# A mixture-of-experts block on one core: y's permit ahead of the gathers, and a weight load that waits for a gather

## The chip, the core and the metric

The kernel runs on one core of a Trainium2 chip. The metric is the device time of one launch in microseconds; runs of the kernel before gave 407.37, 409.26 and 410.68, so the median is 409.26.

## What is computed

The reference is a convolutional attention block over two images of 256 channels and 1024 positions, followed by a dense-looking feed-forward layer with 8 experts in which each of the 2048 tokens has a score for its two best experts and zero for the rest. Only the second part is touched by the change:

```
gate = softmax(xt @ Wg);  topv, topi = top_k(gate, 2);  topv = topv / (sum(topv) + 1e-06)
scores = zeros((T, E)).at[arange(T)[:, None], topi].set(topv)
for e in range(E):
    h = gelu(xt @ W1[e] + b1[e], approximate=False)
    out = out + (h @ W2[e] + b2[e]) * scores[:, e:e + 1]
```

with T = 2048 tokens of 256 values, E = 8, W1 256x1024 and W2 1024x256 for each expert, all in float32. The result is t + out, where t holds the tokens and xt is their layer norm.

## The kernel before

After the attention part (until about 150 us) the kernel sorts the (token, expert) pairs by expert into blocks of 128 rows. A tile is two blocks of one expert; an expert with an odd number of blocks begins with one tile of three. The number of tiles is only known at run time: VectorE writes first tile, end tile and flags of each expert into `bounds`, and each engine reads them into registers (`expert_bounds`, L339). In this run there are 17 tiles, numbered 0 to 16: tiles 0 to 2 are expert 0, 3 to 5 expert 1, 6 expert 2, 7 to 9 expert 3, 10 expert 4, 11 and 12 expert 5, 13 expert 6, 14 to 16 expert 7. Tiles 0 and 11 have three blocks.

Every float32 operand is split into a high and a low part, and each product is three matmuls (hi x hi, lo x hi, hi x lo).

One tile t, engine by engine:

- TensorE (`tile`, L1621): four of the eight first-layer column groups, then second and first layer in turns, then `turn_x(t + 1)` (L1575, transposes at L1572), which waits for `x_gathered` of tile t+1 and transposes the gathered rows `xg` into PSUM; then the last four groups of the second layer. In what follows "the turn in tile t" is this one.
- ScalarE (L813): gelu of each group twice, to h_raw (L820) and h_hi (L823). In the first tile of expert e it also copies the high part of the weights of expert e+1 out of `w_raw` (L833).
- VectorE (L1215): h_lo (L1221) of each group; after the first group of tile t it scales the y of tile t-1 by the scores (`y_scaled`, L1206, y_out at L1212), for which it waits on `y_free`; in an expert's first tile it makes w_lo (L1230); then x_lo (L1203) and y_sum (L1239).
- POOL, that is GpSimd (`tile`, L554): it keeps the scores of tile t+1 (L532, after that gather has landed), waits for the turn in tile t (`xg_turned`), and gathers the rows of tile t+2 into `xg` with three indirect DMAs (`gather`, L515, idx_in at L517, DMAs at L523). Then it waits until every earlier add has landed (`y_added`), copies the destinations into idx_out (L565) and gives `y_free`. When y_out is there (`y_weighted`) it issues two or three indirect DMAs that add y_out to the output rows (L573), and moves the scores on (L537).
- SyncE (L397 to L404): the weights of each expert, two DMAs of 1 MB (`load_expert`, L347), into `w_raw[e % 2]`. The load of expert e waits for `w_split`, that is for the low parts of expert e-2, which VectorE finishes at the end of the first tile of expert e-3; the load of expert 2 waits for the first gather too.

The semaphore of a DMA counts when the transfer has landed, not when it was issued.

Of the kernel before, what the change touches and what calls it, by code (L numbers as in the profile page):

```python
# [34 lines left out]
HJ = H // P  # L35
# [4 lines left out]
WIDE = 3  # L40
# [12 lines left out]
def metaformer_kernel(nc, x_tok_d, q1_d, q2_d, k1_d, k2_d, v_d, o_d, aff_d, og_d, ob_d,  # L53
                      wg_d, w1_d, b1_d, w2_d, b2_d, out_d):
    ctx = ExitStack()
    with ctx:
# [3 lines left out]
        def sem(name):  # L60
            return ctx.enter_context(nc.semaphore(name))
# [223 lines left out]
        bounds_ready = sem("bounds_ready")  # L285
# [7 lines left out]
        x_gathered = sem("x_gathered")  # L293
        idx_in_set = sem("idx_in_set")
        idx_out_set = sem("idx_out_set")
        xg_turned = sem("xg_turned")
# [9 lines left out]
        scores_kept = sem("scores_kept")  # L306
# [6 lines left out]
        w_split = sem("w_split")  # L313
# [25 lines left out]
        def expert_bounds(eng, e):  # L339

            word = eng.value_load(bounds[0:1, 0, bass.ds(e, 1)], min_val=8, max_val=264 * TMAX + 7)
            why = "VectorE counts at most TMAX tiles"
            first = nc.s_assert_within(word // 256, 0, TMAX - 1, skip_runtime_bounds_check_because=why)
            after = nc.s_assert_within(word % 256 // 8, 1, TMAX, skip_runtime_bounds_check_because=why)
            return first, after, word % 8 // 4, word % 2, word % 4 // 2

        def load_expert(sp, e):  # L347
            raw = w_raw[e % 2]
            sp.dma_start(raw[:, 0:KC * H].rearrange("p (k h) -> p k h", k=KC),
                         w1_d[e].rearrange("(k p) h -> p k h", p=P)).then_inc(w_loaded[e % 2], 16)  # L350
            sp.dma_start(raw[:, KC * H:].rearrange("p (j d) -> p j d", j=HJ),
                         w2_d[e].rearrange("(j p) d -> p j d", p=P)).then_inc(w_loaded[e % 2], 16)


        @block.sync
        def _(sp):
            def load_rows(u):
                sp.dma_start(x1[:, u * BLKU:(u + 1) * BLKU, :],
                             x_tok_d[u * UNIT:(u + 1) * UNIT, :].rearrange("(p j) c -> p j c", j=BLKU)
                             ).then_inc(x_loaded[u], 16)  # L360

            load_rows(0)
            load_rows(1)
            sp.dma_start(w_q1[:, :, :], q1_d.rearrange("(k p) o -> p k o", p=P)).then_inc(wq_loaded, 16)
            load_rows(2)
            load_rows(3)
            sp.dma_start(w_q2[:, :], q2_d).then_inc(wq_loaded, 16)
            sp.dma_start(aff[:, :], aff_d).then_inc(wq_loaded, 16)
            for dst, src in ((w_k1, k1_d), (w_v, v_d), (w_g, wg_d)):
                sp.dma_start(dst[:, :, :], src.rearrange("(k p) o -> p k o", p=P)).then_inc(conv_loaded, 16)  # L370
            for dst, src in ((w_k2, k2_d), (w_o, o_d),
                             (og, og_d.partition_broadcast(P)), (ob, ob_d.partition_broadcast(P))):
                sp.dma_start(dst[:, :], src).then_inc(conv_loaded, 16)
            sp.dma_start(b1t[:, :], b1_d).then_inc(bias_loaded, 16)
            load_expert(sp, 0)

            sp.wait_ge(pv_ready, GROUPS)
            sp.dma_start(b2b[:, :], b2_d.partition_broadcast(P)).then_inc(bias_loaded, 16)

            def store_rows(half):  # L380
                sp.wait_ge(xn2_ready, (4, 8)[half])
                sp.wait_ge(xn2_more, (4, 8)[half])
                sp.wait_ge(scores_ready, half + 1)
                sp.dma_start(xs_d[half * HALF * P:(half + 1) * HALF * P, :]
                             .rearrange("(u p j) c -> p u (j c)", p=P, j=BLKU),
                             xn2[:, half * HALF:(half + 1) * HALF, :].rearrange("p (u j) c -> p u (j c)", j=BLKU)
                             ).then_inc(xs_stored, 16)

            store_rows(0)

            sp.wait_ge(x1_ready, NBLK)
            sp.dma_start(out_d[0:TOK, :].rearrange("(u p j) c -> p u (j c)", p=P, j=BLKU),
                         x1[:, :, :].rearrange("p (u j) c -> p u (j c)", j=BLKU)).then_inc(x1_stored, 16)
            store_rows(1)

            sp.wait_ge(lg_ready, NBLK // 2)
            load_expert(sp, 1)  # L397
            for e in range(2, E):

                sp.wait_ge(w_split, HJ * (e - 1))  # L400
                if e == 2:
                    for i in range(WIDE):
                        sp.wait_ge(first_gathered[i], 16)
                load_expert(sp, e)  # L404


        @block.gpsimd
        def _(pool):
# [106 lines left out]
            def gather(n):  # L515

                pool.tensor_copy(idx_in[:, :], row_in[:, bass.ds(n, 1), :].rearrange("p a w -> p (a w)")  # L517
                                 ).then_inc(idx_in_set, 1)
                pool.wait_ge(idx_in_set, n + 1)
                pool.sem_inc(gathers_begun, 1)  # L520
                for i in range(WIDE):
                    done = first_gathered[i] if isinstance(n, int) and n == 0 else x_gathered
                    pool.indirect_dma_start(xg[:, i, :], None, xs_d,  # L523
                                            bass.IndirectOffsetOnAxis(ap=idx_in[:, i:i + 1], axis=0)
                                            ).then_inc(done, 16)

            def keep_scores(n):

                if not (isinstance(n, int) and n == 0):
                    pool.wait_ge(x_gathered, n * (16 * WIDE))  # L530
                pool.sem_inc(scores_begun, 1)
                pool.tensor_copy(score_next[:, :, :], xg[:, :, C:]).then_inc(scores_kept, 1)  # L532

            def move_scores(n):
                pool.wait_ge(scores_kept, n + 1)
                pool.sem_inc(scores_begun, 1)
                pool.tensor_copy(score[:, :, :], score_next[:, :, :]).then_inc(scores_moved, 1)  # L537
# [16 lines left out]
            def tile(t, e, block, width):  # L554


                pool.wait_ge(scores_moved, t + 1)
                keep_scores(t + 1)
                pool.wait_ge(scores_kept, t + 2)
                pool.wait_ge(xg_turned, t + 2)  # L560
                gather(t + 2)


                pool.wait_ge(y_added, block * 16 + 16)
                pool.tensor_copy(idx_out[:, :], row_out[:, bass.ds(t, 1), :].rearrange("p a w -> p (a w)")  # L565
                                 ).then_inc(idx_out_set, 1)
                pool.wait_ge(idx_out_set, t + 1)
                pool.sem_inc(y_free, 1)

                pool.wait_ge(y_weighted, t + 2)  # L570
                pool.sem_inc(adds_begun, 1)
                for i in range(width):
                    pool.indirect_dma_start(out_d, bass.IndirectOffsetOnAxis(ap=idx_out[:, i:i + 1], axis=0),  # L573
                                            y_out[:, i, :], None, compute_op=ALU.add).then_inc(y_added, 16)
                move_scores(t + 1)

            for e in range(E):
                _, t1, odd, more, _ = expert_bounds(pool, e)

                odd1 = pool.value_load(bounds[0:1, 1, e:e + 1], min_val=0, max_val=E)  # L580
                with pool.If(odd):
                    tile(t0, e, t0 * 2 + odd0, WIDE)
                with pool.Else():
                    tile(t0, e, t0 * 2 + odd0, 2)
                with pool.If(more):
                    with pool.Fori(t0 + 1, t1) as t:
                        tile(t, e, t * 2 + odd1, 2)
                t0 = t1
                odd0 = odd1
# [6 lines left out]
        def _(act):  # L596
# [255 lines left out]
            for e in range(E):  # L852
                _, t1, odd, more, _ = experts[e]
                with act.If(odd):
                    tile(t0, e, WIDE, True)
                with act.Else():
                    tile(t0, e, 2, True)
                with act.If(more):
                    with act.Fori(t0 + 1, t1) as t:
                        tile(t, e, 2, False)  # L860
                t0 = t1
# [821 lines left out]
```

## Time and profile before

| | us |
|---|---|
| median of 3 runs (lowest, highest) | 409.26 (407.37, 410.68) |
| the profiled execution | 408.46 |
| its span | 406.7 |
| TensorE busy | 362.1 (89%) |
| VectorE busy | 257.4 (63%) |
| ScalarE busy | 254.4 (63%) |
| GpSimd (POOL) busy | 188.2 (46%) |

Times in the trace are us from the start of the span. The span is what the profiled execution shows of the program; its device time is 1.8 us longer. A row of a timeline gives start, length, engine, line and instruction, and in brackets how long the engine stood idle before it and what ended that. TensorE's clock was granted at full speed throughout the expert part. The DMA issues on SyncE's queue are marked SPq.

### The profile page before, as it was taken

Reading aid. Unit: us, or ns where it says so; the run is one execution under the profiler, and the core shown is the slowest. Engines: PE = TensorE matmul, PEld = TensorE weight load, DVE = VectorE, ACT = ScalarE, POOL = GpSimd, SP = SyncE. Lnnn points to the kernel's source line nnn. Section 1 sums busy time; section 2 is a strip of 40 time slices with the busy share of each in tenths; the row PEclk is TensorE's granted clock in tenths of the full one; section 3 lists DMA queues with packets and bytes.
Section 4 is the critical chain, followed back from the end, with each engine's and each line's share of the span. In section 5 each row is a group of like instructions: output and inputs, shape, how many; then the busy total and the mean of one; then the engine's idle time right before and its main releaser. Section 6 shows DMA issues by size and latency. Waiting matters only on the chain.

```text
span 406.7 us, 8244 instructions
## 1 busy us (share of the span) xinstructions
PE 362.1 (89%) x2500; PEld 324.9 (80%) x2501; DVE 257.4 (63%) x650; ACT 254.4 (63%) x555; POOL 188.2 (46%) x232
## 2 busy tenths in 40 slices
PE   5989978999999796999999899898999999899950
PEld 4435456887879686899999798898989999899950
DVE  5858388788767996554467347784457854935530
ACT  2496657669557764756667466786567855865520
POOL 5800000002025655435666556685657556766553
PEclk9999999999999878999999999999999999999995
DMA  7810000000002773718325631658224714232342
GB/s 272 262 39 2 0 1 2 0 2 0 1 16 92 309 267 95 245 58 229 61 49 133 169 63 42 161 146 266 54 52 90 210 42 71 36 66 55 54 65 27
DMA packets 22965, 38.62 MB, mean 95 GB/s; under 512 B 2576, under 2 KB 17296, under 8 KB 22800
## 3 DMA queue, kind: packets, MB, share of 16 engines
q1 hardware_dynamic: 14896, 25.41, 17.9%
q0 software_dynamic: 8032, 12.82, 17.9%
q14 instruction: 27, 0.22, 0.2%
q8 instruction: 10, 0.16, 0.2%
HBM read 28.85 MB, written 9.37 MB: 94 GB/s over the span
## 4 chain that ended last, share of the span: by engine, by line
PE 51%; DVE 12%; POOL 12%; issue 11%; ACT 6%; DMA 3%; POOLq 2%; DVEq 1%; ACTq 0%
PE banks L1273 8%; PE banks L1275 8%; PE banks L1274 8%; PE banks L1613 5%; PE banks L1617 5%; PE banks L1615 5%; POOL xg L523 5%; POOL out_rows L573 4%; PE banks L1388 3%; PE banks L1311 3%; DMA xg<-xn_rows,idx_in 3%; ACT prob L677 2%; DVE y_out L1212 1%; PE banks L1572 1%; DVE expx L917 1%
## 5 line engine op out<-in xcount | busy, mean ns | idle before, releaser
L820 ACT ACTIVATE h_raw<-banks,b1t 128x256 f32<-128x256 f32 (+1 forms) x136 | 68.3, 502 | 76.0 <-PE banks L1275 76.0
L1221 DVE TENSOR_TENSOR h_lo<-h_raw,h_hi 128x256 fp32r<-128x256 f32 (+1 forms) x136 | 58.5, 440 | 70.8 <-ACT h_hi L823 70.0
L573 POOL DMA_INDIRECT out_rows<-y_out,idx_out x36 | 72.5, 2014 | 42.3 <-DVE y_out L1212 36.5
L1273 PE MATMUL banks<-x_hi,w_hi 128*128 128x256 f32 (+1 forms) x272 | 79.6, 293 | 7.2 <-issue 3.7
L1613 PE MATMUL banks<-w_hi,h_hi 128*128 128x256 f32 x288 | 83.5, 290 | 2.1 <-DVE h_lo L1221 2.0
L1615 PE MATMUL banks<-w_lo,h_hi 128*128 128x256 f32 x288 | 81.4, 283 | 0.0
L1617 PE MATMUL banks<-w_hi,h_lo 128*128 128x256 f32 x288 | 81.4, 283 | 0.0
L1274 PE MATMUL banks<-x_lo,w_hi 128*128 128x256 f32 (+1 forms) x272 | 78.6, 289 | 0.0
L1275 PE MATMUL banks<-x_hi,w_lo 128*128 128x256 f32 (+1 forms) x272 | 78.6, 289 | 0.0
L523 POOL DMA_INDIRECT xg<-xn_rows,idx_in x57 | 58.4, 1024 | 27.9 <-POOL idx_in L517 16.3
L823 ACT ACTIVATE h_hi<-banks,b1t 128x256 fp32r<-128x256 f32 (+1 forms) x136 | 68.2, 502 | 0.0
L1273 PEld LDWEIGHTS banks<-x_hi,w_hi 128*128 128x128 f32 x272 | 52.0, 191 | 9.1 <-issue 9.1
L1613 PEld LDWEIGHTS banks<-w_hi,h_hi 128*128 128x128 f32 x288 | 55.1, 191 | 3.3 <-DVE h_lo L1221 3.0
L1615 PEld LDWEIGHTS banks<-w_lo,h_hi 128*128 128x128 f32 x288 | 55.1, 191 | 0.0
L1617 PEld LDWEIGHTS banks<-w_hi,h_lo 128*128 128x128 f32 x288 | 55.1, 191 | 0.0
L1274 PEld LDWEIGHTS banks<-x_lo,w_hi 128*128 128x128 f32 x272 | 52.1, 191 | 0.0
L1275 PEld LDWEIGHTS banks<-x_hi,w_lo 128*128 128x128 f32 x272 | 52.0, 191 | 0.0
L475 POOL TENSOR_SCALAR rstd<-x_square 128x4 f32<-128x4 f32 x4 | 1.0, 247 | 100.5 <-ACT xn L706 100.5
L1230 DVE TENSOR_TENSOR w_lo<-w_raw,w_hi 128x512 fp32r<-128x512 f32 x56 | 38.6, 688 | 1.4
L833 ACT ACTIVATE w_hi<-w_raw 128x512 fp32r<-128x512 f32 x56 | 37.7, 672 | 0.0
L686 ACT ACTIVATE pt_hi<-banks 128x512 fp32r<-128x512 f32 x32 | 17.4, 594 | 15.5 <-PE banks L1388 15.5
L947 DVE TENSOR_REDUCE rmax<-banks 128x1 f32<-128x1024 f32 x16 | 19.6, 1223 | 7.8 <-PE banks L1275 7.8
(219 smaller groups left out, 663.5 us busy)
## 6 DMA issues: line engine op xcount, KB each, us to landing
w_raw<-in_w SPq DMA_DIRECT2D x16, 1024.0 KB, 8.0
xn_rows<-xn SPq DMA_DIRECT2D x2, 1056.0 KB, 4.7
x<-in_x_tok SPq DMA_DIRECT2D x4, 512.0 KB, 5.1
out_rows<-x SPq DMA_DIRECT2D x1, 2048.0 KB, 9.3
b2b<-in_b SPq DMA_DIRECT2D x1, 1024.0 KB, 4.7
xg<-xn_rows,idx_in POOLq DMA_INDIRECT x57, 3.6
out_rows<-y_out,idx_out POOLq DMA_INDIRECT x36, 3.9
out_rows<-x POOLq DMA_DIRECT2D x1, 384.0 KB, 3.2
```

The source lines that it names most:

```text
L523: pool.indirect_dma_start(xg[:, i, :], None, xs_d, bass.IndirectOffsetOnAxis(ap=idx_in[:, i:i + 1], axis=0)).then_inc(done, 16)
L573: pool.indirect_dma_start(out_d, bass.IndirectOffsetOnAxis(ap=idx_out[:, i:i + 1], axis=0), y_out[:, i, :], None, compute_op=ALU.add).then ...
L820: act.activation(h_raw[j % RING][:, 0:w], banks[:, j % RING, 0:w], ACT.Gelu, bias=bias)
L823: act.activation(h_hi[:, j, 0:w], banks[:, j % RING, 0:w], ACT.Gelu, bias=bias).then_inc(gelu_done, 1)
L1221: dve.tensor_tensor(h_lo[:, j, 0:w], h_raw[j % RING][:, 0:w], h_hi[:, j, 0:w].bitcast(F32), ALU.subtract).then_inc(h_split, 1)
L1230: dve.tensor_tensor(w_lo[(e + 1) % 2][:, c], w_raw[(e + 1) % 2][:, c], w_hi[(e + 1) % 2][:, c].bitcast(F32), ALU.subtract).then_inc(w_spli ...
L1273: pe.matmul(out, a_hi, b_hi, start=start, stop=False)
L1274: pe.matmul(out, a_hi, b_lo, start=False, stop=False)
L1275: return pe.matmul(out, a_lo, b_hi, start=False, stop=stop)
L1613: pe.matmul(out, h_hi[:, j, r], w_hi[e % 2][:, c], start=j == 0 and i < 2, stop=False, skip_group_check=width == WIDE)
L1615: pe.matmul(out, h_hi[:, j, r], w_lo[e % 2][:, c], start=False, stop=False, skip_group_check=width == WIDE)
L1617: ins = pe.matmul(out, h_lo[:, j, r], w_hi[e % 2][:, c], start=False, stop=j == HJ - 1, skip_group_check=width == WIDE)
```

## The change

On GpSimd, in `tile`, the wait for `y_added`, the copy to idx_out and `y_free` move ahead of the waits for `xg_turned` and the gather. On SyncE the load of expert e, for e from 3, waits in addition for a gather: `first` is the first tile of expert e-3, and the value stands for the gather of tile `first + 2` having landed, which POOL issues in tile `first`. SyncE reads `first` out of `bounds` for that.

```diff
             sp.wait_ge(lg_ready, NBLK // 2)
             load_expert(sp, 1)
+            sp.wait_ge(bounds_ready, 2)
             for e in range(2, E):
 
-                sp.wait_ge(w_split, HJ * (e - 1))
                 if e == 2:
+                    sp.wait_ge(w_split, HJ)
                     for i in range(WIDE):
                         sp.wait_ge(first_gathered[i], 16)
+                else:
+                    first = expert_bounds(sp, e - 3)[0]
+                    sp.wait_ge(w_split, HJ * (e - 1))
+
+                    sp.wait_ge(x_gathered, (first + 2) * (16 * WIDE))
                 load_expert(sp, e)
...
                 pool.wait_ge(scores_moved, t + 1)
                 keep_scores(t + 1)
-                pool.wait_ge(scores_kept, t + 2)
-                pool.wait_ge(xg_turned, t + 2)
-                gather(t + 2)
-
 
                 pool.wait_ge(y_added, block * 16 + 16)
                 pool.tensor_copy(idx_out[:, :], row_out[:, bass.ds(t, 1), :].rearrange("p a w -> p (a w)")
                                  ).then_inc(idx_out_set, 1)
                 pool.wait_ge(idx_out_set, t + 1)
                 pool.sem_inc(y_free, 1)
+                pool.wait_ge(scores_kept, t + 2)
+                pool.wait_ge(xg_turned, t + 2)
+                gather(t + 2)
```

Line numbers of the changed kernel are 5 or 6 higher than before from GpSimd's part on. The order of instructions on GpSimd in a two-block tile, before:

```order
L532 COPY score_next<-xg 128x24 [waits scores_moved,x_gathered]
L517 COPY idx_in<-row_in 128x3 [waits xg_turned,scores_kept]
L523 DMA xg<-xn_rows,idx_in 128x264 [waits idx_in_set]
L523 DMA xg<-xn_rows,idx_in 128x264 x2
L565 COPY idx_out<-row_out 128x3 [waits y_added]
L573 DMA out_rows<-y_out,idx_out 2432x256 [waits idx_out_set,y_weighted]
L573 DMA out_rows<-y_out,idx_out 2432x256
L537 COPY score<-score_next 128x24 [waits scores_kept]
```

The same tile in the changed kernel:

```order
L538 COPY score_next<-xg 128x24 [waits scores_moved,x_gathered]
L567 COPY idx_out<-row_out 128x3 [waits y_added]
L523 COPY idx_in<-row_in 128x3 [waits idx_out_set,xg_turned,scores_kept]
L529 DMA xg<-xn_rows,idx_in 128x264 [waits idx_in_set]
L529 DMA xg<-xn_rows,idx_in 128x264 x2
L578 DMA out_rows<-y_out,idx_out 2432x256 [waits y_weighted]
L578 DMA out_rows<-y_out,idx_out 2432x256
L543 COPY score<-score_next 128x24 [waits scores_kept]
```

idx_out and its wait for y_added now stand ahead of the three gathers; the adds stand where they stood. On SyncE, the loads of experts 2, 3 and 4 before:

```order
L349 DMA w_raw<-in_w 128x2x1024 [waits first_gathered1,first_gathered2,first_gathered0,w_split]
L351 DMA w_raw<-in_w 128x8x256
L349 DMA w_raw<-in_w 128x2x1024 [waits w_split]
L351 DMA w_raw<-in_w 128x8x256
L349 DMA w_raw<-in_w 128x2x1024 [waits w_split]
L351 DMA w_raw<-in_w 128x8x256
```

The loads of experts 2 and 3 in the changed kernel:

```order
L349 DMA w_raw<-in_w 128x2x1024 [waits first_gathered1,first_gathered0,first_gathered2,w_split,bounds_ready]
L351 DMA w_raw<-in_w 128x8x256
L341 TENSOR_LOAD bounds
L341 ISA x2
L409 ISA [waits w_split]
L349 DMA w_raw<-in_w 128x2x1024 [waits x_gathered]
L351 DMA w_raw<-in_w 128x8x256
```

Each load from expert 3 on has gained a read of bounds ahead of w_split and the wait for x_gathered behind it.

## Rows read from the trace of the kernel before

**Rows 1.** TensorE in order of time: turns of xg (L1572), and h_lo waits.

```profile
189.99 0.60 PE L1572 MATMUL banks<-ident,xg 128*128 128x128 f32 x4
...
198.10 0.39 PE L1613 MATMUL banks<-w_hi,h_hi 128*128 128x256 f32 x1 [0.31 <-DVE h_lo L1221]
...
202.51 0.60 PE L1572 MATMUL banks<-ident,xg 128*128 128x128 f32 x4
...
230.14 0.66 PE L1572 MATMUL banks<-ident,xg 128*128 128x128 f32 x4 [1.72 <-DMA xg<-xn_rows,idx_in]
...
277.92 0.39 PE L1613 MATMUL banks<-w_hi,h_hi 128*128 128x256 f32 x1 [0.90 <-DVE h_lo L1221]
...
282.86 0.66 PE L1572 MATMUL banks<-ident,xg 128*128 128x128 f32 x4 [0.37 <-issue]
...
294.87 0.60 PE L1572 MATMUL banks<-ident,xg 128*128 128x128 f32 x4
```

**Rows 2.** The waits: VectorE's y_out held by y_free (us, times, longest).

```profile
DVE y_out L1212 <- POOLq L568: 7.8, 12, 1.8
```

**Rows 3.** POOL in order of time: gathers L523, adds L573, a whole cycle from 283.76.

```profile
181.27 0.95 POOL L523 DMA_INDIRECT xg<-xn_rows,idx_in  x1 [0.30 <-issue]
...
189.16 1.56 POOL L573 DMA_INDIRECT out_rows<-y_out,idx_out  x1 [0.30 <-issue]
...
221.25 0.96 POOL L523 DMA_INDIRECT xg<-xn_rows,idx_in  x1 [0.30 <-issue]
...
264.24 4.07 POOL L573 DMA_INDIRECT out_rows<-y_out,idx_out  x1 [1.91 <-DVE y_out L1212]
...
283.76 0.19 POOL L517 COPY idx_in<-row_in 128x3 uint32 x1 [0.67 <-PE banks L1572]
284.79 1.04 POOL L523 DMA_INDIRECT xg<-xn_rows,idx_in  x1 [0.84 <-POOL idx_in L517]
...
287.42 0.95 POOL L523 DMA_INDIRECT xg<-xn_rows,idx_in  x1 [0.30 <-issue]
288.38 0.20 POOL L565 COPY idx_out<-row_out 128x3 uint32 x1
290.48 1.75 POOL L573 DMA_INDIRECT out_rows<-y_out,idx_out  x1 [1.90 <-DVE y_out L1212]
292.53 1.58 POOL L573 DMA_INDIRECT out_rows<-y_out,idx_out  x1 [0.30 <-issue]
...
294.59 0.41 POOL L532 COPY score_next<-xg 128x24 f32<-128x24 f32 x1 [0.25 <-POOL score L537]
295.71 0.19 POOL L517 COPY idx_in<-row_in 128x3 uint32 x1 [0.72 <-PE banks L1572]
```

**Rows 4.** SyncE's queue in order of time: two of the weight loads, first half.

```profile
219.55 0.37 SPq L349 DMA_DIRECT2D w_raw<-in_w  x1
...
272.80 0.37 SPq L349 DMA_DIRECT2D w_raw<-in_w  x1
```

**Rows 5.** DMA issues, median us to landing, at 297, 287, 273, 221, 293, 225.

```profile
xg<-xn_rows,idx_in POOLq DMA_INDIRECT x3, 2.9
...
xg<-xn_rows,idx_in POOLq DMA_INDIRECT x1, 3.6
...
xg<-xn_rows,idx_in POOLq DMA_INDIRECT x3, 6.1
...
xg<-xn_rows,idx_in POOLq DMA_INDIRECT x1, 8.4
...
out_rows<-y_out,idx_out POOLq DMA_INDIRECT x1, 3.8
...
out_rows<-y_out,idx_out POOLq DMA_INDIRECT x2, 5.6
```

**Rows 6.** POOL in order of time at the end: the adds of tiles 15 and 16.

```profile
386.34 1.60 POOL L573 DMA_INDIRECT out_rows<-y_out,idx_out  x1 [0.30 <-issue]
...
396.25 1.63 POOL L573 DMA_INDIRECT out_rows<-y_out,idx_out  x1 [1.90 <-DVE y_out L1212]
```

## Prediction

> **What bounds the kernel now.** I read the page first, then TensorE's stretches between its four-matmul turns of xg (one turn per tile, so their spacing is the pace), then POOL in order of time, then the landings of its DMAs.
>
> From the first turn on, TensorE is the clock of the kernel. An undisturbed two-block tile runs from turn to turn in 294.87 - 282.86 = 12.0 us [rows 1]. Some tiles are longer because a new expert begins (registers and branches); the change doesn't touch that. Three places are longer because of what it does touch [rows 1]: 198.10, TensorE idle 0.31 for h_lo; 230.14, the turn idle 1.72 for a gather; 277.92 and 282.86, idle 0.90 for h_lo and 0.37 at the turn. Behind the h_lo waits stands VectorE held by y_free, 12 times and 7.8 us in all [rows 2]; most of these 12 are absorbed, since TensorE lost time at two only. Behind the turns stand gathers that ran beside a weight load.
>
> POOL's cycle [rows 3]: idx_in at 283.76, gathers 284.79 to 288.38, idx_out, adds at 290.48 and 292.53, the next tile's score_next at 294.59, the next idx_in at 295.71. Only the last of these waits for TensorE (0.72 idle), so POOL has some 0.7 us to spare in 12 and more than that nowhere. This decides the case.
>
> SyncE issues loads at 219.55 and 272.80 [rows 4], in the middle of POOL's gathers. DMA [rows 5]: free gathers land in 2.9 us in the median and 3.6 for the third; a median of 6.1 just behind the load of 272.80, and 8.4 for the one at 221.25 behind the load of 219.55. Adds land in 3.8 when alone, and in 5.6 when issued 5 to 7 us into a load. No row shows an add issued in the first 4 us of a load.
>
> **Part 1, idx_out and y_free ahead of the gather.** y_added counts landings, not issues. Before, idx_out stood behind the gather and found every earlier add landed (no idle at 288.38). Now the gather stands behind that wait. In the free cycle: the second add starts at 292.53 and lands 3.8 later, 296.3; wake, idx_out copy and hand-over take about 0.5 (an estimate from the 0.19 copy and the 0.25 idle between two POOL copies [rows 3]); idx_in to first gather is 1.03 [rows 3]. The gather starts near 297.9 where it started near 296.7. So it is about 1.2 us later in each tile, and y_free comes about 4 us earlier.
>
> Two chains follow, all from [rows 3, 5]. From the landing of the adds to the turn that needs the gather: 0.5 + 1.0 + 2.6 (first to third gather) + 3.6 + 0.5 (turn after landing: 221.25 + 8.4 = 229.65 to 230.14) = 8.2 us. The adds of tile t must have landed 8.2 us ahead of the turn in tile t+2. And POOL's own loop, add to add: 2.05 + 3.8 + 0.5 + 1.0 + 3.6 + a gap of 0.3 (between two DMA issues) to 0.8 (idx_in to gather) = 11.3 to 11.8 us. Before, it was 4.1 to score_next, 0.6, 1.0, 3.6, then y_free, y_out and 0.8, about 11.4. The loop is no shorter and still fits in 12.0 by a hair. So part 1 alone costs nothing in a free stretch, takes the h_lo stalls away, and lets a late add delay a gather, which it could not do before.
>
> Gains of part 1: at the turn of 202.51 the pace was 12.52 and becomes 12.0, -0.5. At 277.92 the 0.90 goes [rows 1], with a restart about -1.1. At the tail POOL now gathers (a gather nobody uses) before the last adds instead of before y_free: the adds of 386.34 land at 390.1, plus 1.5 plus 3.6 gives a gather end at 395.3, plus 0.3 to 0.8 gives last adds at 395.6 to 396.1 for 396.25 [rows 6], -0.4.
>
> **Part 2, the load waits for the gather.** SyncE issues nothing else in this stretch, so nothing is queued behind its wait. Its added reads of bounds stand before the w_split wait, where it idles for tens of us. The loads of experts 3 to 7 move from the end of a tile to the landing of that tile's third gather, 5 to 8 us later. Their splits come at the earliest one expert later, so no load is late (each has over 12 us). Gathers in that tile land in 3.6 again: the 1.72 goes, and the 0.37 with its restart, together -2.3 (1.87 and 0.5). All gains: 0.5 + 1.1 + 0.4 + 2.3 = 4.3 us.
>
> **What they cost together.** The load that no longer meets the gathers now starts about when the second add is issued, and that add gates the next gather. An add in a load loses between 0 (bound below: its few packets slip in ahead) and 3.2 (6.1 against 2.9, gathers right behind a load [rows 5]; 8.4 against 3.6 for the single worst one, 4.8, is the far end); late in a load it is 5.6 - 3.8 = 1.8. I take 2.4, between the two, since the second add falls at the front but with part of its way already done.
>
> - Load of expert 3, at 181.27 + 3.6 = 184.9. The third add of tile 0 is issued at 189.16 [rows 3], 4.3 into it, so I use 1.8: landed 194.8, turn possible at 203.0. Natural turn: 202.0. So 0.5 later than now.
> - Load of expert 4. TensorE's next natural turns: 202.51 to 230.14 less the 1.87 is 25.8, so 228.8, 1.3 earlier than now. POOL by its loop: adds landed near 206.4 and (slow issue) 219.4, gather landed 227.1, in time. Its load starts there; tile 3's second add starts near 226.2 and lands at 230.0 + 2.4 = 232.4. Needed: 228.8 + 12.0 - 8.2 = 232.6. Just in time.
> - Loads of experts 5 and 6, one tile apart. Tile 6's adds: TensorE's time gives 264.24 - 1 = 263.2, POOL's loop 262 to 264. Their issue is slow in a tile that splits weights (4.07 at 264.24 where 1.75 is usual [rows 3], and perhaps less when it comes later), so the second starts 3 to 4.4 later, at 266 to 268, the load at 265. Landed 272.5 to 275, turn possible at 280.7 to 283.2, natural 280.3. The load of expert 6 starts there with tile 7's adds at 278 to 281, landed 286 to 289 with the 2.4, turn possible 294.5 to 297.5. Now it is at 294.87. So -0.4 to +2.6, middle +1.1.
> - Load of expert 7 falls beside a three-block tile of 16.7 us: nothing. Nothing later recovers or loses: all tiles are at TensorE's pace.
>
> A rule bears on this. [Rows 5] show 6.1 to 8.4 for gathers behind a load. The Trainium skill (DMA: Bandwidth & Descriptors, Queues, rings and completion order) says each DMA engine takes turns between queues a whole packet at a time. The trace agrees for gathers. By it an add at the front of a load would pay what a gather pays, which is the third rival below.
>
> **Sum.** +1.1 at the turn of 294.87, -0.4 at the tail: +0.7. The profiled execution took 408.46 (span 406.7); the median of the three runs is 409.26. 409.26 + 0.7 gives 410.0. The gain and the price are each near 4 to 5 us, and their difference is small and uncertain.
>
> **Rivals.**
> - *The adds slip ahead of the load* (delay under about 1 us). For it: they are two or three small transfers, and the first is issued 2 us ahead of the load. Against: 5.6 for adds late in a load. All gains stay: 409.26 - 4.3 = 405.0. Chance 0.2.
> - *A late add holds the next gather at the full price*: slower. Place: gathers of tiles 5, 9 and 10 (after the loads of experts 3 to 6). Price 3.2 or more instead of 2.4, in three consecutive links (loads 4, 5, 6): 3 x 0.8 = 2.4, plus 0.5 for the loop gap at 0.8 instead of 0.3 in each of four cycles, 2: +0.7 + 4.4 = +5.1, so 414.4. It decides once the delay passes about 3 us. For it: the gathers' 6.1 and 8.4. Against: slow issues of 4.07 may be shorter when they come later, which gives back 1 us each. Chance 0.24.
> - *A weight load comes too late for its split* and ScalarE waits: each load has more than an expert's tile in hand, by 10 us and more. It would give 415 and up. Chance 0.02.
> - Forecast: both effects near balance, 408 to 413. Chance 0.54.
>
> About 1% is what a measurement of this kernel can tell from no change: below 405.2 or above 413.3. Faster takes 0.14, most of the first rival; slower takes 0.24 of the second and third and a little of the forecast, 0.26; the rest, 0.60, is the same. The range is 404.7 to 415: from the full gain to the second rival.
>
> **What would show it.** Right: y_out's idle for y_free near zero; gathers issued about 1 us after the adds land and no longer after the turn; gathers of the tiles that a load follows landing in 3.6; adds beside the loads in 5.5 to 7; TensorE idle at the turns near 203, 282 and 296. Wrong: adds beside loads still in 4 us (then 405), or gathers still issued right after the turn, or an idle of ScalarE at w_hi for a load.

## The result, and the profile after

The changed kernel takes 419.41 us in the median of 6 runs (418.19 to 422.22), against 407.75 for the kernel before in the same jobs (407.29 to 410.68, 6 runs). The ratio is 1.0277, with a 95% interval of 1.0232 to 1.0322: 11.3 us slower. The prediction was 410.0 with a range up to 415.0. The mechanism that it feared is there; its price is three times what it was given.

The profiled execution took 420.03, its span is 418.3. The turns of xg on TensorE (L1577 now) show where the time went. The columns are those of [rows 1].

```profile
178.08 0.60 PE L1577 MATMUL banks<-ident,xg 128*128 128x128 f32 x4
191.46 0.60 PE L1577 MATMUL banks<-ident,xg 128*128 128x128 f32 x4
...
207.03 1.12 PE L1577 MATMUL banks<-ident,xg 128*128 128x128 f32 x4 [2.89 <-DMA xg<-xn_rows,idx_in]
...
220.52 0.60 PE L1577 MATMUL banks<-ident,xg 128*128 128x128 f32 x4
...
233.04 0.60 PE L1577 MATMUL banks<-ident,xg 128*128 128x128 f32 x4
...
248.08 1.12 PE L1577 MATMUL banks<-ident,xg 128*128 128x128 f32 x4 [2.78 <-DMA xg<-xn_rows,idx_in]
...
261.79 0.60 PE L1577 MATMUL banks<-ident,xg 128*128 128x128 f32 x4
275.23 0.60 PE L1577 MATMUL banks<-ident,xg 128*128 128x128 f32 x4
289.83 0.66 PE L1577 MATMUL banks<-ident,xg 128*128 128x128 f32 x4 [1.91 <-DMA xg<-xn_rows,idx_in]
...
305.85 1.12 PE L1577 MATMUL banks<-ident,xg 128*128 128x128 f32 x4 [2.98 <-DMA xg<-xn_rows,idx_in]
...
399.99 0.60 PE L1577 MATMUL banks<-ident,xg 128*128 128x128 f32 x4
```

Four turns wait 10.6 us for gathers, where the kernel before waited 1.72 and 0.37 [rows 1]. From the first turn to the 17th it is 399.99 - 178.08 = 221.9 us; before it was 388.67 - 176.60 = 212.1. That is 9.8 of the 11.6 us between the two spans (418.3 and 406.7). Of the rest, 1.5 lies ahead of the first turn: it came between 176.0 and 180.7 in the profiles of this study, and nothing of the change acts there. So I compare traces by this stretch from here on, and times by their ratios.

GpSimd in order of time shows what each of the four is made of. This is tile 3, whose gather releases the load of expert 4; the load is the second fence, from SyncE's queue.

```profile
228.49 1.62 POOL L578 DMA_INDIRECT out_rows<-y_out,idx_out  x1 [0.95 <-DVE y_out L1217]
230.42 1.60 POOL L578 DMA_INDIRECT out_rows<-y_out,idx_out  x1 [0.30 <-issue]
...
232.48 0.20 POOL L538 COPY score_next<-xg 128x24 f32<-128x24 f32 x1 [0.25 <-POOL score L543]
239.10 0.19 POOL L567 COPY idx_out<-row_out 128x3 uint32 x1 [6.41 <-DMA out_rows<-y_out,idx_out]
239.69 0.19 POOL L523 COPY idx_in<-row_in 128x3 uint32 x1 [0.40 <-POOL idx_out L567]
240.73 1.52 POOL L529 DMA_INDIRECT xg<-xn_rows,idx_in  x1 [0.85 <-POOL idx_in L523]
```

```profile
230.35 0.37 SPq L349 DMA_DIRECT2D w_raw<-in_w  x1
```

The add of 228.49 is issued 1.9 us ahead of the load and lands in 3.8. The add of 230.42 starts with the load and lands in 8.5. GpSimd stands idle for 6.41 us, most of it with the turn of 233.04 done, and the gather goes out at 240.73 where the turn that needs it could have been at 233.04 + 12.0 = 245.0. The issues (last figure: median us to landing) of the adds at 228.49, 230.42, 190.62 and 288.87; the last two are 4.1 us after and 0.45 us before their loads:

```profile
out_rows<-y_out,idx_out POOLq DMA_INDIRECT x1, 3.8
...
out_rows<-y_out,idx_out POOLq DMA_INDIRECT x1, 8.5
...
out_rows<-y_out,idx_out POOLq DMA_INDIRECT x1, 7.1
...
out_rows<-y_out,idx_out POOLq DMA_INDIRECT x1, 7.6
```

The waits (total us, times, longest) name the new bound, and show that what was meant to go did go in part: VectorE's wait for y_free has fallen from 7.8 us and 12 times [rows 2] to 3.8 and 4.

```profile
POOL idx_out L567 <- DMA out_rows<-y_out,idx_out: 41.8, 16, 6.4
POOL out_rows L578 <- DVE y_out L1217: 12.7, 9, 3.1
PE banks L1577 <- DMA xg<-xn_rows,idx_in: 10.6, 4, 3.0
...
DVE y_out L1217 <- POOLq L570: 3.8, 4, 1.5
```

One more price stands in the windows: the tile after a long idle is slower. The columns are the window, its length, busy us of TensorE, its weight load, VectorE, ScalarE and GpSimd with instruction counts, then TensorE's granted clock, the busy share of the DMA engines and GB/s.

```profile
207.00:216.00 9.00, 8.97 (x63) 8.95 (x64) 3.95 (x10) 4.01 (x9) 4.32 (x9) 0.82 0.27 54
248.00:257.00 9.00, 8.86 (x61) 8.66 (x62) 3.69 (x9) 3.75 (x9) 4.50 (x8) 0.82 0.27 52
305.00:314.00 9.00, 8.15 (x54) 8.03 (x55) 2.95 (x7) 3.01 (x7) 5.22 (x8) 0.81 0.36 59
```

After the idles of 2.89, 2.78 and 2.98 the granted clock is at 1.2 instead of 2.4 GHz for a part of each window (a mean of 0.81 to 0.82), and the turn itself takes 1.12 instead of 0.60. After the idle of 1.91 the turn takes 0.66.

### The profile page after: what moved, and what is told of

Its sections match the earlier page's. It is cut to its first block, busy times and chain, and to the rows that moved or that the text cites. A ratio compares the mean times of both kernels' runs of the same rounds, so it can differ in the third digit from the quotient of the medians.

```text
span 418.3 us, 8264 instructions
## 1 busy us (share of the span) xinstructions
PE 369.0 (88%) x2500; PEld 332.8 (80%) x2501; DVE 258.1 (62%) x650; ACT 254.7 (61%) x555; POOL 178.4 (43%) x232
## 4 chain that ended last, share of the span: by engine, by line
PE 42%; issue 13%; DMA 12%; DVE 12%; ACT 9%; POOL 7%; POOLq 1%; DVEq 1%; ACTq 0%
DMA out_rows<-y_out,idx_out 9%; PE banks L1278 7%; PE banks L1280 6%; PE banks L1279 6%; PE banks L1618 4%; PE banks L1620 4%; PE banks L1622 4%; DMA xg<-xn_rows,idx_in 3%; PE banks L1393 3%; POOL xg L529 3%; PE banks L1316 3%; POOL out_rows L578 2%; ACT h_hi L828 2%; ACT prob L682 1%; ACT w_hi L838 1%
## 5 line engine op out<-in xcount | busy, mean ns | idle before, releaser
L1618 PE MATMUL banks<-w_hi,h_hi 128*128 128x256 f32 x288 | 85.1, 295 | 1.8 <-DVE h_lo L1226 1.8
L1620 PE MATMUL banks<-w_lo,h_hi 128*128 128x256 f32 x288 | 82.8, 288 | 0.0
L1622 PE MATMUL banks<-w_hi,h_lo 128*128 128x256 f32 x288 | 82.6, 287 | 0.0
L529 POOL DMA_INDIRECT xg<-xn_rows,idx_in x57 | 60.5, 1061 | 27.8 <-POOL idx_in L523 16.3
L578 POOL DMA_INDIRECT out_rows<-y_out,idx_out x36 | 61.4, 1705 | 22.7 <-DVE y_out L1217 12.7
L1618 PEld LDWEIGHTS banks<-w_hi,h_hi 128*128 128x128 f32 x288 | 56.7, 197 | 2.6 <-DVE h_lo L1226 2.5
L1620 PEld LDWEIGHTS banks<-w_lo,h_hi 128*128 128x128 f32 x288 | 56.7, 197 | 0.0
L1622 PEld LDWEIGHTS banks<-w_hi,h_lo 128*128 128x128 f32 x288 | 56.5, 196 | 0.0
L1208 DVE TENSOR_TENSOR x_lo<-banks,x_hi 128x768 fp32r<-128x768 f32 x17 | 16.3, 958 | 16.1 <-ACT x_hi L815 15.8
```

Source lines behind the costliest of these rows:

```text
L529: pool.indirect_dma_start(xg[:, i, :], None, xs_d, bass.IndirectOffsetOnAxis(ap=idx_in[:, i:i + 1], axis=0)).then_inc(done, 16)
L1618: pe.matmul(out, h_hi[:, j, r], w_hi[e % 2][:, c], start=j == 0 and i < 2, stop=False, skip_group_check=width == WIDE)
L1620: pe.matmul(out, h_hi[:, j, r], w_lo[e % 2][:, c], start=False, stop=False, skip_group_check=width == WIDE)
L1622: ins = pe.matmul(out, h_lo[:, j, r], w_hi[e % 2][:, c], start=False, stop=j == HJ - 1, skip_group_check=width == WIDE)
```

## The experiments

Three theories stood at the start. A: the two parts meet. The load that waits for the gather starts with the adds, the adds land late, and the moved y_added wait passes that on to the next gather. B: the moved wait alone costs it. C: holding the loads costs it.

### GpSimd's part alone

This is the kernel before with GpSimd's part of the diff alone; SyncE releases the loads as it did before.

> Only GpSimd's part of the change; SyncE issues the loads as before. Theory A (the two parts meet: the load released by the gather starts as the adds are issued, the adds land 3.5 to 5 us later, and the moved y_added wait passes that on to the next gather): here the loads start 5 us ahead of the adds, which land in 4 to 6, so the time is near the kernel before, -1 to +3 us, and the turns near 230 and 283 still wait for gathers behind a load. Theory B (the moved wait alone costs it: every gather starts later and POOL's loop no longer fits into a tile): +8 us or more, with turns waiting in most tiles.

Measured: 410.64, ratio 1.0036 (0.9995 to 1.0078), +1.5 us. From first to 17th turn 390.09 - 177.06 = 213.0, 1.0 more than before. The waits:

```profile
POOL idx_out L561 <- DMA out_rows<-y_out,idx_out: 23.9, 16, 1.8
...
PE banks L1571 <- DMA xg<-xn_rows,idx_in: 4.7, 3, 2.2
```

The same 16 waits of idx_out are there, but none is above 1.8 us. B falls. Two of the three turns that wait have a gather behind a load, as A says: 1.69 us at 229.56 and 2.24 at 282.95. The third has no load near it:

```profile
346.98 3.39 POOL L523 DMA_INDIRECT xg<-xn_rows,idx_in  x1 [0.30 <-issue]
```

```profile
353.50 0.66 PE L1571 MATMUL banks<-ident,xg 128*128 128x128 f32 x4 [0.72 <-DMA xg<-xn_rows,idx_in]
```

The last load had started at 313.65. This gather took 3.39 us to issue instead of 1, beside VectorE's h_lo and w_lo at the start of a tile that splits weights. So the moved order has a small price of its own here, 0.72 us at one turn, which the traces of the change and of the cut loads below don't show.

### SyncE's part alone

GpSimd's part of the diff is undone: gather first, then y_added, idx_out and y_free.

> Only SyncE's part of the change; GpSimd gathers before it waits for y_added, as before. Theory A: the adds beside a load land in 7 to 9 us here too, but no gather waits for them; only y_free is late, by 1 to 3 us, so no turn waits for a gather, a few h_lo waits of about 1 us stand in their place, and the time is -2 to +1.5 us of the kernel before. Theory B: the same. Theory C (holding the loads is what costs, since they slow whatever follows them, or are late for ScalarE): +5 us or more.

Measured: 406.30, ratio 0.9937 (0.9904 to 0.9969), -2.6 us; C falls. From first to 17th turn 390.54 - 180.74 = 209.8, 2.3 less than before. Here is the same place as above, in the old order. First GpSimd:

```profile
228.51 1.66 POOL L579 DMA_INDIRECT out_rows<-y_out,idx_out  x1 [1.90 <-DVE y_out L1218]
230.47 1.60 POOL L579 DMA_INDIRECT out_rows<-y_out,idx_out  x1 [0.30 <-issue]
...
233.32 0.19 POOL L523 COPY idx_in<-row_in 128x3 uint32 x1 [0.29 <-PE banks L1578]
234.36 1.04 POOL L529 DMA_INDIRECT xg<-xn_rows,idx_in  x1 [0.85 <-POOL idx_in L523]
...
237.93 0.20 POOL L571 COPY idx_out<-row_out 128x3 uint32 x1
```

Then the landing of these two adds; the load started at 229.30:

```profile
out_rows<-y_out,idx_out POOLq DMA_INDIRECT x2, 7.2
```

The adds are late here too: the second lands at 230.47 + 7.2 = 237.7. Nothing waits for it, since the gathers went out from 234.36 on and idx_out stands behind them, at 237.93 and without idle. Only behind the load of expert 6 does idx_out wait in this trace, 0.59 us at 290.74. A late add costs next to nothing in one order and a stall in the other. No turn from the first on waits for a gather.

### The loads taken away, in both orders

The loads of experts 3 to 7 are cut to two small pieces, so those experts compute with partly stale weights. The same edit is made to the changed kernel and to the one before.

```diff
+        def load_little(sp, e):
+            raw = w_raw[e % 2]
+            sp.dma_start(raw[:, 0:16], w1_d[e, 0:P, 0:16]).then_inc(w_loaded[e % 2], 16)
+            sp.dma_start(raw[:, KC * H:KC * H + 16], w2_d[e, 0:P, 0:16]).then_inc(w_loaded[e % 2], 16)
...
-                load_expert(sp, e)
+                if e == 2:
+                    load_expert(sp, e)
+                else:
+                    load_little(sp, e)
```

> The changed kernel, with the weight loads of experts 3 to 7 cut from 2 MB to two pieces of 128x16 (those experts compute with weights that are partly stale). Theory A: the adds land in 3.8 everywhere, no turn waits for a gather, and all gains stay: 4 us below the kernel before. Theory B: still 8 us or more above it, since the moved wait is there in every tile.

> The kernel before with the same cut of the loads of experts 3 to 7 (those experts compute with weights that are partly stale). Theory A: the 1.72 and 0.37 us of idle at the turns go, the h_lo waits of 0.31 and perhaps 0.9 stay: 2 to 3 us below the kernel before, and 1 to 2 us above the changed kernel with cut loads. Theory B: at least 8 us below the changed kernel with cut loads.

Measured: 405.80 in the changed kernel, ratio 0.9929 (0.9890 to 0.9969), and 406.22 in the kernel before, 0.9933 (0.9900 to 0.9966). That is -2.9 and -2.7 us, where I had expected 4 and 2 to 3. By their times the two can't be told apart, because the stretch ahead of the first turn scatters by more. From first to 17th turn the traces do: 207.1 and 209.5 (387.41 - 177.93). The first and the last turn of the changed kernel with cut loads:

```profile
176.48 0.60 PE L1585 MATMUL banks<-ident,xg 128*128 128x128 f32 x4
...
383.56 0.60 PE L1585 MATMUL banks<-ident,xg 128*128 128x128 f32 x4
```

So without the loads the changed kernel is 5.0 us below the kernel before in this stretch, with them 9.8 above. The loads cost it 14.8 us; they cost the kernel before 2.6. This is A again. It also gives the change's gain its true size: 2.4 us for the moved order (209.5 to 207.1), and 2.6 for gathers free of loads. Each of these stretches is from one trace; the two traces of the next experiment give 207.6 and 207.3 in the moved order again.

### The load released by the adds

If A holds, the moment of release decides. In the changed kernel the load is held until the adds of the expert's first tile have landed.

```diff
-                    first = expert_bounds(sp, e - 3)[0]
+                    first, _, odd, _, _ = expert_bounds(sp, e - 3)
+                    odd0 = sp.value_load(bounds[0:1, 1, e - 4:e - 3], min_val=0, max_val=E) if e > 3 else 0
                     sp.wait_ge(w_split, HJ * (e - 1))
-                    sp.wait_ge(x_gathered, (first + 2) * (16 * WIDE))
+                    sp.wait_ge(y_added, first * 32 + odd0 * 16 + odd * 16 + 48)
```

> The changed kernel, with the loads of experts 3 to 7 held until the adds of the expert's first tile have landed, instead of its gather. Theory A: the adds land in 4 to 5 again, but the load now starts 1.5 us ahead of the next gather, whose third part lands in 6.5 to 8.4 instead of 3.4. In the moved order a gather has only about 2 us in hand, so a turn waits 1 to 3 us for each of the loads that no long tile covers: +3 to +8 us of the kernel before. If only the meeting with the adds mattered and a gather could bear a load as it did in the kernel before: -2 to 0 us.

Measured: 404.47, ratio 0.9907 (0.9876 to 0.9938). My expectation of +3 to +8 was wrong: it is -3.8 us. One release, 4 to 8 us later for experts 3 to 5 (counted from the turn before it), turns 11.3 us slower into 3.8 faster. The third gather behind the load of 194.80, and the turn that needs it:

```profile
199.24 0.96 POOL L529 DMA_INDIRECT xg<-xn_rows,idx_in  x1 [0.30 <-issue]
```

```profile
204.59 0.66 PE L1577 MATMUL banks<-ident,xg 128*128 128x128 f32 x4 [0.58 <-DMA xg<-xn_rows,idx_in]
```

The third gather, 4.4 us into the load, must have landed about 0.5 ahead of the turn, so in about 4.9 us (an estimate, with the 0.5 between landing and turn of the prediction; this trace has no landing for it). I had given it 6.5 to 8.4, from gathers issued within 2.5 us of a load's start. This is the only turn of the 17 that waits.

Once more, beside the same release in the old order:

> The changed kernel with the load held until the adds of the expert's first tile have landed, once more, beside the one above: -3 to -4.5 us of the kernel before.

Measured: 404.45, ratio 0.9927 (0.9903 to 0.9951), -3.0 us.

> GpSimd as before; the loads of experts 3 to 7 held until the adds of the expert's first tile have landed. Theory A: a load now starts within 1 us of the next gather's first part, which lands in 6 to 7, but the old order gives that gather 3 to 4 us more time, so no turn waits over 1 us; y_free finds its adds landed: the h_lo waits of 0.3 and 0.9 stay. -3 to 0 us of the kernel before, and 1 to 3 us above the same hold in the moved order. If instead the moved order gives nothing of its own: no more than 0.5 us above it.

Measured: 406.11, ratio 0.9965 (0.9937 to 0.9993), -1.4 us. From first to 17th turn 387.18 - 177.16 = 210.0, against 383.31 - 176.03 = 207.3 for the moved order. So the moved order gives 2.7 us of its own, close to the 2.4 without loads: the h_lo waits of [rows 1] remain in the old order and one turn waits 0.54.

### The loads in halves

W1 is released by the gather as in the change, W2 by the gather of the tile after, in the moved order and, as a third form of the hold, in the old one.

```diff
                     sp.wait_ge(x_gathered, (first + 2) * (16 * WIDE))
-                load_expert(sp, e)
+                    load_half(sp, e, 0)
+                    sp.wait_ge(x_gathered, (first + 3) * (16 * WIDE))
+                    load_half(sp, e, 1)
+                if e == 2:
+                    load_expert(sp, e)
```

> The changed kernel, with each load of experts 3 to 7 in two halves: W1 released by the gather as now, W2 by the gather of the tile after. Theory A: an add waits for what is queued of the load, and 1 MB alone lands in 5, so the last adds land in 5 to 6.5 instead of 7 to 9; the turns wait 0 to 2 us where they waited 2 to 3: +1 to +6 us of the kernel before. If the delay of an add does not depend on the length of the load: +10 us and more, since twice as many adds meet a load.

> Only SyncE's part, in the same two halves; GpSimd as before. Theory A: no gather meets a load and no turn waits; the adds land in 5 to 6.5, ahead of the idx_out that waits for them, so y_free is no later than in the kernel before: -2.5 us of it (-4 to -1), 0 to 1 us below the hold alone.

> The changed kernel with the loads in halves, once more, for its profile: +14 to +20 us of the kernel before. Adds issued within 0.5 us of either half land in 7 to 8.5, those issued 2 us or more into a half in 4 to 5, and some gathers behind a late add take 4 us or more to issue because they fall into the dense stretch of VectorE at the start of a tile that splits weights.

Measured: in the moved order 427.05, ratio 1.0444 (1.0396 to 1.0493), and in the second job 426.98 in 2 runs, 1.0471 (1.0429 to 1.0513); in the old order 406.99, 0.9977 (0.9950 to 1.0005). The last is -0.9 us by the ratio, just short of the -4 to -1 expected, and not below the hold of whole loads; its stretch from first to 17th turn is 386.96 - 176.71 = 210.2, against 209.8 for that hold. For the moved order I had first expected +1 to +6 us, because 1 MB alone lands in 5; it is +18 to +19. The profile is that of the second job. Its waits:

```profile
POOL idx_out L580 <- DMA out_rows<-y_out,idx_out: 45.9, 16, 7.1
PE banks L1590 <- DMA xg<-xn_rows,idx_in: 14.5, 5, 4.5
```

The two possibilities that my expectation set against each other can be told apart in the trace of the old order, which has the landings. This add was issued 1.2 us into a W1 half:

```profile
226.46 1.60 POOL L592 DMA_INDIRECT out_rows<-y_out,idx_out  x1 [0.30 <-issue]
```

```profile
out_rows<-y_out,idx_out POOLq DMA_INDIRECT x1, 5.6
```

Three adds at 1.2 to 1.3 us into a half took 5.6 to 5.8, where the add at the same place of a whole load, 230.47 above, took 7.2. So the length of the load does matter for an add issued behind its start. For adds issued 0.7 to 0.9 us ahead of a half it hardly does: they took 6.8 to 7.0, where the one of 228.51, 0.8 ahead of a whole load, took 7.2.

The slowdown comes from where the second halves fall. Turns of xg in the moved order, behind a W1 half, a W2 half, a W1 half and a W2 half:

```profile
202.21 0.66 PE L1590 MATMUL banks<-ident,xg 128*128 128x128 f32 x4
...
219.63 1.11 PE L1590 MATMUL banks<-ident,xg 128*128 128x128 f32 x4 [4.47 <-DMA xg<-xn_rows,idx_in]
...
246.42 0.66 PE L1590 MATMUL banks<-ident,xg 128*128 128x128 f32 x4
...
262.94 0.84 PE L1590 MATMUL banks<-ident,xg 128*128 128x128 f32 x4 [3.40 <-DMA xg<-xn_rows,idx_in]
```

The two turns behind a W1 half, which waited 2.89 and 2.78 us behind a whole load, show no wait, and the third waits 1.15 instead of 1.91. But a W2 half is released by the next gather, and four of the five start 0.4 to 0.7 us behind the start of the last add, which then lands late too. GpSimd at the first of these stalls, beside the W2 half that started at 201.70 and landed in 5.7:

```profile
201.02 1.59 POOL L591 DMA_INDIRECT out_rows<-y_out,idx_out  x1 [0.30 <-issue]
...
208.25 0.30 POOL L580 COPY idx_out<-row_out 128x3 uint32 x1 [4.97 <-DMA out_rows<-y_out,idx_out]
...
209.99 3.94 POOL L542 DMA_INDIRECT xg<-xn_rows,idx_in  x1 [0.86 <-POOL idx_in L536]
```

The add of 201.02, 0.7 us ahead of 1 MB, releases idx_out at 208.25, so it took 7 us. And the gather behind it takes 3.94 us to issue instead of 1.04, and at three of these four W2 halves such a gather takes 3.0 to 3.9. VectorE then makes h_lo and w_lo back to back:

```profile
209.51 0.68 DVE L1248 TENSOR_TENSOR w_lo<-w_raw,w_hi 128x512 fp32r<-128x512 f32 x1
210.11 0.42 DVE L1239 TENSOR_TENSOR h_lo<-h_raw,h_hi 128x256 fp32r<-128x256 f32 x1
210.45 0.68 DVE L1248 TENSOR_TENSOR w_lo<-w_raw,w_hi 128x512 fp32r<-128x512 f32 x1
```

An issue of GpSimd's in this dense stretch is slow, as the 4.07 of an add in [rows 3] was. The Trainium skill (SBUF — State Buffer, SBUF: two separate sides) says that during some of VectorE's ops, an fp32 copy for one, GpSimd is locked out of a port that the two share and can't write a DMA's descriptors. The ops in these rows are subtractions and not that copy; the times fit such a lock, and no run here separates it from another cause.

The last expectation was right in the time and in the slow gathers, and in part wrong in the landings. The trace of the moved order has no landings for most of these adds, but the start of idx_out, which waits for the last add, bounds them: the add 0.3 us into a half (337.19) took at most 6, not 7 to 8.5, and the add of 289.41 about 9; two halves, of experts 5 and 6, started behind it, at 289.80 and 290.90. The add 4.3 us into a half (189.26) took at most 4, as expected.

## Why the prediction was wrong

Release of the load against order, each as the ratio to the kernel before in its own job:

| load of experts 3 to 7 released by | old order | moved order |
|---|---|---|
| w_split (end of the tile) | 1 | 1.0036 |
| the gather's landing | 0.9937 | 1.0277 (the change) |
| the adds' landing | 0.9965 | 0.9927, 0.9907 |

GpSimd's part alone moves the time by +1.5 us (its interval takes in zero), SyncE's by -2.6, the two together by +11.3. The interaction is the whole of it.

- *Gains.* Predicted 3.9 us without the tail, measured 5.0 (207.1 against 212.1, loads cut): 2.4 for the moved order, where I had 1.6, and 2.6 for gathers free of loads, where I had 2.3. Right. The tail gave nothing that a trace shows: 18.3 us from the 17th turn to the end of the span, 18.0 before.
- *The gather about 1.2 us later in a free cycle, POOL's loop within 12.0.* Right, but for one turn: with the loads cut no turn waited, and in GpSimd's part alone the turn of 353.50 waited 0.72 behind a gather with a slow issue. I had counted slow issues for adds only.
- *The chain from the adds' landing to the turn, 8.2 us.* Too short, and the smaller of the two steps that failed. It was 9.3, 9.2, 8.8 and 9.4 at the four stalls (the second: landed at 238.9, turn at 248.08). There idx_in came 0.8 after the landing, where I had 0.5 for wake, copy and hand-over together, and the third gather 3.1 after the first, where I had 2.6, since the first took 1.52 to issue instead of 1.04.
- *"An add in a load loses between 0 and 3.2 ... I take 2.4."* This is the step that failed first of all, and the larger one. The last adds ahead of the four stalls took 7.1, 8.5, 7.1 (the second add of tile 6, 2.6 us into its load, with its slow issue) and 7.6. That is 3.3, 4.7, 2.7 and 3.8 more than they take alone (3.8, or 4.4 for the slow one). All but the third are above the 3.2 that I had from the gathers [rows 5]. The 3.3 is that of the add 4.1 us into the first load, for which I had used 1.8, the price of an add late in a load; this load landed only 11.7 us after its start. Against my 1.8, 2.4, 2.4 and 2.4 the four lost 1.5, 2.3, 0.3 and 1.4 more, 5.5 in all; the chain was 0.6 to 1.2 too short each time, 3.9 in all.
- *The three links.* After the load of expert 3 I had the turn 1.0 behind its natural time, it was 207.03 - (191.46 + 12.0) = 3.6. After that of expert 4 I had "just in time", it was 248.08 - (233.04 + 12.0) = 3.0. After those of experts 5 and 6 it was 2.1 and 4.0 (289.83 against 275.23 + 12.5, where 12.5 is that tile with the loads cut, and 305.85 against 289.83 + 12.0). In all 12.7. I had about 5 in all: 1.0, 0 and some 4 for the last two. At the first two the misses explain the difference to 0.1: 1.5 and 1.1 make the 2.6 that the first lacked; 2.3 and 1.0, less the 0.2 that I had in hand, the 3.0 of the second. Since I stood at the deadline with almost nothing in hand, what the add and the chain took beyond my values went for the most part into a turn.
- *What was not in the sum.* TensorE's clock. Each of the three tiles after the long idles took 0.7 us more than with the loads cut (13.49, 13.71 and 13.70 against 12.78, 13.04 and 13.02), 2.1 us. With the 12.7 that makes the 14.8 that the loads cost; my price was 5.0.
- *The rivals.* The second one (the full price) was right in its place, its chain and its sign; its 414.4 was too low, since "full price" meant 3.2 there and was up to 4.7, the chain was too short and the clock was missing. That ScalarE would wait for a load did not come.
- *The rule.* That an engine takes turns between queues a whole packet at a time (the Trainium skill, DMA: Bandwidth & Descriptors, Queues, rings and completion order) was cited for the higher price. The traces agree in direction: adds around the front of a load lost 2.7 to 4.8 us, about what gathers lost behind one (3.2 to 4.8 in [rows 5]). I let it only shape a rival, the second of the list, and sized the sum by a value between that row and zero for which no row spoke.

The change is not wrong in either of its ideas. Its load is released at the one moment when the moved order can't bear it. Held one step longer it is 0.7 to 0.9% below the kernel before, the fastest correct version of this study.

## What to carry to other kernels

When a wait on a landing is moved ahead of an issue, every transfer that the landing counts gets onto the critical path; ask next what will run beside those transfers, above all if the same change moves a load. If a large load has to meet something, let it meet transfers that nobody waits for (here the adds in the old order) or start it when the awaited ones have landed. And a cost that no row shows is to be taken from the nearest row, not from between that row and zero, when the sum has no slack left to absorb it. That alone would not have been enough here: with 3.2 I had 414.4, and the rest was a chain taken too short and the clock.

## What the runs showed of the hardware

- How late an indirect add lands beside a load of 2 MB depends on where it starts. In the change it took 3.8 at 1.9 us ahead of the load, 7.6 to 8.6 within 0.5 us of its start, 7.1 to 7.8 at 1.6 to 2.6 us into it, and 7.1 at 4.1 us into it; at 5 to 7 us into it 5.6 [rows 5]. Two adds at 3.7 and 5.7 us into a load took 6.7 and 6.5 in GpSimd's part alone. An issue that is slow itself comes on top: the add of 270.54, 0.8 us ahead of its load, took 3.1 us to issue and 9.1 to land.
- With 1 MB instead of 2 MB an add 1.2 us into the piece took 5.6 instead of 7.2; 0.7 to 0.9 us ahead of it 6.8 to 7.0 instead of 7.2.
- Idles of TensorE of 2.8 to 3.0 us were followed by a stretch at 1.2 GHz that cost 0.7 us in the next tile, on top of the idle itself; the ones of 1.7 (the kernel before) and 1.9 us were not. The 2.24 us in GpSimd's part alone was followed by one too, in which the clock was 0.81 over the next 9 us; after the 4.47 in the run with halves it was 0.63.
